# Attention inside a two-layer kernel: products with the values for two steps at a time, a ring of twelve tiles of exponentials, no zeros sent into loaded query stacks

## The reference, cut to what matters

```
q, k, v = (proj(Wq, bq), proj(Wk, bk), proj(Wv, bv))
...
q = q * cos + rotate_half(q) * sin
k = k * cos + rotate_half(k) * sin
...
attn = jnp.einsum('bhqd,bhkd->bhqk', q, k) * scale
attn = jax.nn.softmax(attn, axis=-1)
out = jnp.einsum('bhqk,bhkd->bhqd', attn, v)
```

## Time and profile before

| what | value |
|---|---|
| median of 3 runs | 977.3 us (977.19 to 978.48) |
| the profiled execution | 978.52 us |
| its span in the trace | 976.7 us |
| TensorE busy | 801.6 us, 82% of the span |
| VectorE busy | 818.1 us, 84% |
| ScalarE busy | 668.0 us, 68% |
| attention's eight passes | 77.6 us to 446.9 us of the span |

### The profile page before, as it was taken

How to read it: one execution, slowest core, us unless ns; L and a number is a source line. 1 busy time by engine, 2 the same in 40 slices (tenths; PEclk the granted TensorE clock), 3 DMA queues, 4 the chain that set the end, 5 groups by cost and what they waited for, 6 DMA issues and landing times.

```text
span 976.7 us, 13030 instructions
## 1 busy us (share of the span) xinstructions
PE 801.6 (82%) x4241; PEld 414.7 (42%) x4241; DVE 818.1 (84%) x764; ACT 668.0 (68%) x1233; POOL 239.6 (25%) x132
## 2 busy tenths in 40 slices
PE   4579989999999999986375475677665679999998
PEld 2312212221222222223353355555554548888886
DVE  6788858887888888895888889999999846888886
ACT  2305757776777777775133597999994368888885
POOL 3800000000000000010100057888987501221220
PEclk9857979999999999999778688999999579999999
DMA  8422321212022110001200234455552021221221
GB/s 187 114 65 61 82 76 34 61 34 64 31 70 79 47 53 12 12 12 39 64 0 6 86 110 154 152 198 190 202 205 90 0 90 61 69 66 64 65 65 43
DMA packets 41524, 76.05 MB, mean 78 GB/s; under 512 B 7560, under 2 KB 25456, under 8 KB 40432
## 3 DMA queue, kind: packets, MB, share of 16 engines
q1 hardware_dynamic: 41464, 75.30, 24.7%
HBM read 64.99 MB, written 8.85 MB: 76 GB/s over the span
## 4 chain that ended last, share of the span: by engine, by line
PE 54%; ACT 17%; DVE 17%; issue 5%; SPq 4%; DMA 1%; POOL 0%; ACTq 0%; DVEq 0%; POOLq 0%
PE ps L1441 12%; PE ps L1462 11%; ACT dtb L912 8%; PE ps L1412 6%; PE ps L1696 6%; PE ps L1697 6%; PE ps L1698 6%; ACT abar L886 5%; DVE nmax L1066 3%; DVE hst L1201 2%; PE ps L1513 1%; SPq L521 1%; SPq L531 1%; DVE fx L454 1%; DVE fx L455 1%
## 5 line engine op out<-in xcount | busy, mean ns | idle before, releaser
L789 ACT ACTIVATE prob<-ps 128x512 f32<-128x512 f32 x512 | 265.0, 605 | 114.5 <-PE ps L1441 112.1
L1069 DVE TENSOR_REDUCE nmax_k<-ps 128x2 f32<-128x1024 f32 x224 | 262.4, 1219 | 45.5 <-PE ps L1412 44.3
L1441 PE MATMUL ps<-qs,ks 96*128 96x512 bf16 x512 | 165.8, 396 | 8.3 <-ACT prob L789 3.8
L717 POOL TENSOR_TENSOR hc<-hst,cbr 128x1024 f32<-128x1024 f32 x64 | 154.6, 2438 | 35.3 <-DVE hst L1201 23.7
L1201 DVE TENSOR_TENSOR_SCAN hst<-abar,ps 128x1024 f32<-128x1024 f32 x64 | 142.8, 2273 | 4.0 <-ACT abar L886 2.1
L1462 PE MATMUL ps<-prob,vq 128*16 128x512 f32 x1024 | 135.9, 608 | 0.8 <-ACT prob L789 0.7
L1284 DVE TENSOR_TENSOR act_l<-act_t,act_h 128x1024 fp32r<-128x1024 f32 x64 | 91.0, 1431 | 37.2 <-ACT act_h L996 37.2
L1441 PEld LDWEIGHTS ps<-qs,ks 96*128 96x128 bf16 x512 | 40.1, 98 | 169.5 <-ACT prob L789 109.0
L992 ACT ACTIVATE act_t<-ps,b_now 128x512 f32<-128x512 f32 x128 | 82.9, 683 | 25.4 <-PE ps L1698 25.4
L912 ACT ACTIVATE dtb<-dtxt,bt 128x128 f32<-128x128 f32 x328 | 99.8, 389 | 0.0
L1611 PE MATMUL ps<-ident,dtb 128*128 128x128 f32 x328 | 50.4, 291 | 51.2 <-DVE hst L1201 41.6
(11 more groups left out here) (192 smaller groups left out, 1146.6 us busy)
## 6 DMA issues: line engine op xcount, KB each, us to landing
cbr<-s_dram SPq DMA_DIRECT2D x64, 512.0 KB, 4.2
gate<-c_dram SPq DMA_DIRECT2D x8, 1024.0 KB, 7.5
qs<-q_dram SPq DMA_DIRECT2D x16, 288.0 KB
ks<-k_dram SPq DMA_DIRECT2D x48, 96.0 KB
o_dram<-o_sb SPq DMA_DIRECT2D x16, 256.0 KB, 2.0
wf<-in_L_ffn_w SPq DMA_DIRECT2D x8, 256.0 KB, 2.8
wfq<-in_L_ffn_w SPq DMA_DIRECT2D x8, 256.0 KB, 3.1
km<-k_dram SPq DMA_DIRECT2D x56, 32.0 KB
```

Source lines behind the costliest of these rows:

```text
L717: nc.gpsimd.tensor_tensor(hc[:, slot], hst[:, slot], cbr[:, slot], ALU.mult).then_inc(s_hc, 1)
L789: nc.scalar.activation(prob[:, n % 8], ps[:, 4 + (first + n) % 3], ACT.Exp, scale=ATT_SCALE).then_inc(s_exp, 1)
L1069: nc.vector.tensor_reduce(nmax_k[:, half, kk, 2 * pair:2 * pair + 2, qt], ps[:, 2 * pair:2 * pair + 2, :], AX.X, ALU.max, negate=True).the ...
L1441: nc.tensor.matmul(ps[:, 4 + (first + n) % 3], ks[p][:, kt // 4, j, kt % 4 * P:(kt % 4 + 1) * P], qs[p][:, half, j, :], start=True, stop=T ...
```

## The change

The ring of exponentials has 12 tiles in place of 8 (10 in `prob`, 2 in the new `prob_2`, in whose memory `fill` now lies as well). ScalarE's wait for a free place in the ring names the products three steps back in place of two. TensorE issues the products of two steps together, after the last score of an even step (ahead of the last score where there are no pairs); step 15 does those of step 14, and its own follow. The transfer of zeros at the end of `load` goes, and `LOADS` counts one transfer less.

```
-        fill = sb("fill", [4 * (ROWS - PROD), 2, 2 * BANK], BF16)
+        prob_2 = sb("prob_2", [P, 2, BANK])
+        fill = prob_2[0:4 * (ROWS - PROD)].bitcast(BF16)
...
-        prob = sb("prob", [P, 8, BANK])
+        prob = sb("prob", [P, 10, BANK])
...
+        def prob_at(n):
+
+            n = n % 12
+            return prob[:, n] if n < 10 else prob_2[:, n - 10]
...
-        LOADS = 16 * (2 * (PARTS + 1) + 1)
+        LOADS = 16 * 2 * (PARTS + 1)
...
-                sp.dma_start(qs[p][PROD:PROD + 2], fill[0:16, 0, 0:BANK]).then_inc(s_qk[p], 16)
...
-                        if j == 0 and s >= 2:
-
-                            act.wait_ge(s_pv, STEPS * it + s - 1)
+                        if j == 0 and s >= 3:
+
+                            act.wait_ge(s_pv, STEPS * it + s - 2)
                         act.wait_ge(s_st, 4 * STEPS * it + n + 1)
-                        nc.scalar.activation(prob[:, n % 8], ps[:, 4 + (first + n) % 3], ACT.Exp,
+                        nc.scalar.activation(prob_at(n), ps[:, 4 + (first + n) % 3], ACT.Exp,
...
-                        if s >= 1 and j == (QUAD - 1 if todo else QUAD - 2):
-                            products(it, p, s - 1)
+                        if j == (QUAD - 1 if todo else QUAD - 2):
+                            if s % 2 == 0 and s >= 2:
+                                products(it, p, s - 2)
+                                products(it, p, s - 1)
+                            elif s == STEPS - 1:
+                                products(it, p, s - 1)
```

More of the change, by code:

```diff
@@ L1461, in products @@
                 for j in range(QUAD):
-                    mm = nc.tensor.matmul(ps[32 * j:32 * j + VW, 7], vq[p][:, kt, j, :], prob[:, (4 * s + j) % 8],
+                    mm = nc.tensor.matmul(ps[32 * j:32 * j + VW, 7], vq[p][:, kt, j, :], prob_at(4 * s + j),
                                           start=(kt == 0), stop=(kt == KT - 1))
```

## The result

The changed kernel takes 983.33 us (median of 5 runs, 982.74 to 985.46) against 977.3 (976.17 to 978.48 in the 5 runs beside them): 0.7% slower, ratio 1.0069 with a 95% interval of 1.0056 to 1.0082. Forecast were 984.3 us, and slower. The profiled execution took 985.12 us, 983.3 of them span, which is 6.6 above the span before.

The account below looks back on a forecast made before the run. TensorE, without gaps, was taken as the bound, VectorE and ScalarE close behind. Passes 2 to 6 5.0, pass 0 0, pass 1 0.8, last pass 1.6, zeros -0.4: 7.0 us on 977.3 gives 984.3, range 979.3 to 987.8.

Parts of the forecast that it names:

- The steps: In a steady pair of steps, TensorE waits 0.26 us more against 0.11 saved by joined products: 0.15 us longer.
- The row of 5.55 us: Starts within a steady pair of steps, from first score to the next pair at 5.55 us, where two steps took 5.40.
- A pass: A whole attention pass becomes 1.07 us longer: 0.25 in its first three steps, 0.75 and 0.07 in later pairs.
- The zeros: Dropping the transfer of zeros at the end of a load gains between 0 and 0.69 us, taken as 0.4.
- Pass 0 and its cover: Pass 0 ends in a 3.06 us wait for stored maxima through SyncE's queue, hiding its slower steps: cost 0.
- pass 1 starts at the lower clock after that wait: Pass 1 begins at the lower clock after pass 0's 3.06 us wait, so only later pairs count: 0.8 us.
- the rival to which I gave 10%: The clock stays up in pass 1 because the idle before it shrinks by 1 us: 979.7 us; chance 10%.
- the stated range: The whole time, leaving out no more than 2 in 10: from 979.3 to 987.8 us.
- the third rival: Pairs of steps lose a further 0.08 us, or the last pass falls to the lower clock: 988 us; chance 14%.
- The last pass's structure: The last pass costs 1.6 us: 1.7 at steps 12 and 14, 0.2 for steps 6 to 11, less 0.3.

Follow-up runs that it names:

- e1_zeros_only: The kernel before with only the transfer of zeros at the end of a load left out: 975.02 us against 975.01, ratio 1.0003.
- e4_ring_only: The changed kernel (ring of twelve, no zeros) with products of one step at a time as before: 975.13 us, ratio 0.9994 to before.
- e6_last_single_again: The changed kernel with products of one step at a time in the last pass alone, second run: 983.28 us, ratio 1.0060 to before.
- e9_half_both: The changed kernel with exponentials over half of each scores tile and reductions over half of each bank: a pair of steps took 5.28 us.

## Why the prediction was right

**The steps.** The bound was read rightly: TensorE without gaps, ScalarE and VectorE so near behind it that 8 scores in a row make it wait more (0.26) than the joined products save (0.11). The row of 5.55 us stood in the trace as it was summed, and the three runs with halved work show each part by itself: 0.11 to 0.12 saved with neither engine in the way, and a wait for either of the two. So the mechanism of the steps is shown by runs.

**A pass.** 1.07 us was forecast and 1.16 and 1.07 measured in passes 2 and 4. The pairs of steps in pass 6 took 5.58 where before they took 5.52, so that pass cost 0.5 alone, which the forecast took for a full one. In pass 4 the parts fit as well: 7.81 us for the first three steps as forecast, and 5.80 for steps 9 and 10 (forecast 5.75). Steps 7 and 8 took 5.64 where 5.55 was forecast, and step 15, which was to stay, took 3.56 in place of 3.64.

**The zeros.** The term of 0.4 us was wrong in size: nothing was gained, the lower bound that the text named, as the key loads issued just ahead land as late. The row names the last transfer issued as the one that ended the wait, and taking it away made nothing earlier.

**Pass 0 and its cover.** Right: the slower steps cost nothing there, because SyncE's queue sets its end. Moreover pass 0 became 0.9 us shorter, but most of that is not the double products': with single products it took 49.13 and 49.00 us in e1_zeros_only and e4_ring_only against 49.86 before and 48.94 in the changed kernel. SyncE's queue starts from the store of the maxima for the pass's second half, and how soon that comes hangs on the stretch at the lower clock with which pass 0 begins. That stretch ended 5.8 us into the pass before, and the store was issued 17.29 us into it. Where it ended equally early (4.9 us), the store came at 16.83 with single products (e1_zeros_only) and at 16.49 with double ones (e6_last_single_again). So about 0.3 us can be due to the products, as in a block of steps the pairs follow each other without products between them; that reason is argued, not shown.

**Pass 1.** The step that failed in the profiled execution is "pass 1 starts at the lower clock after that wait": the rival to which I gave 10% came true in seven further profiles with double products in pass 0. The one exception is e9_half_both, whose faster pass 0 ended in a pause of 2.99 us again (its step 15 took 6.61 us, 3.56 without a pause) and was followed by the low clock. With the reordered queue neither the pause nor the low clock is there. So in these profiles the clock of pass 1 goes with the length of the pause. That was 5.2 us to the good against the forecast (-4.4 in place of +0.8). The rival's own sum of 979.7 left out that the forecast had added 0.8 us to pass 1: by its terms it should have been 978.9, just below the stated range.

**Passes 3 and 7.** The forecast was kept near by what went the other way: 2.4 us of lower clock in pass 3 (3.5 less the 1.07 of the steps) and 2.8 in pass 7 (49.99 us against 47.24 at full clock). This too had been named, in the third rival, for the last pass alone. The last pass's structure, 1.6 us forecast, measured 1.4: steps 12 and 14 each took 0.86 more (0.87 forecast), and step 12 began 0.33 us earlier (33.80 us into the pass in place of 34.13), where the forecast had 0.1.

The total was thus right with its mechanism, and its closeness to 984.3 is in part luck: clock terms of 5.2 us on one side and 5.2 on the other cancel.

## What to carry to other kernels

When three engines are within a quarter of each other, joining work on the one that bounds lengthens the others' pauses and then their bursts; put the new block together from starts, waits and the number of buffers that feed the neighbour (three banks of scores here), not from the drain that is saved. A longer ring behind an engine does not help if what it starves for is ahead of it. And before tuning a step, look at the pauses between stages: one pause of 3 us, made by the order in a queue, cost 3.1 us itself and 5.5 of lower clock behind it in the profiles (the new order saved 5 to 6 us of the whole time), and slower steps that happened to fill it hid much of their own price (6 us with it in the way, 15.9 without, by the medians).

## What the runs showed of the hardware

A pause of TensorE of 2.8 to 3.1 us ahead of pass 1 was followed by the lower clock for 13.7 us in four profiles out of four (before, e1_zeros_only, e4_ring_only, e9_half_both), one of 1.0 to 1.4 us in none of eight. In pass 3 all fourteen profiles have a pause of 1.9 to 2.4 us and the lower clock for 3.4 to 10.2 us with it. In the kernel before, ScalarE starts late there, for no reason that the profile shows, and TensorE waits for it:

```profile
223.45 4.03 ACT L789 ACTIVATE prob<-ps 128x512 f32<-128x512 f32 x8 [2.02 <-issue]
224.11 0.39 PE L1441 MATMUL ps<-qs,ks 96*128 96x512 bf16 x1 [2.16 <-ACT prob L789]
```

That pass took 47.5 us where its neighbours took 43.8 and 43.9, so the pause and the lower clock with it cost 3.6 us, and no experiment here touched them.

The Trainium skill, TensorE: Matmul & The Clock Gate, Part 1, has it that being throttled is the default state and that activity releases it. The trace of before agrees: the granted clock was 0.50 from 68 us on, where TensorE waited 0.2 to 0.8 us after every four matmuls, and became 1.00 at 83.4 us, 5.8 us into the gapless work of pass 0. But in pass 7 the same program had a clock of 1.00 in one execution (47.24 us) and 0.93 in another (49.99), and pass 3 had between 0.90 and 0.96. Behind attention, where the code is the same in all kernels, the time from the last copy to the end was 529.5 to 530.1 us in all six profiles with single products in passes 1 to 7, and 529.4 to 534.8 in the eight others. What decides between them no run here shows. It sets how well a change of some us can be read from whole times.
